# Heads of 8 in an attention kernel: single steps against woven rounds of two, with the PSUM banks shared out anew

## The reference, cut to what matters

```
q, k, v = x @ Wq, ctx @ Wk, ctx @ Wv        # 16 heads of width 8
p       = softmax(q @ k.T * 8 ** -0.5)      # 256 queries x 1601 keys
out     = concat_heads(p @ v) @ Wo + x
```

## Time and profile before

| | |
|---|---|
| time, median of 3 runs | 7700.89 us (7677.93 to 7725.98) |
| the profiled execution | 7682.88 us, its span 7681.1 us |
| heads-of-8 stages, first exp to last, `a0` | 1478 us |
| the same, `a1` and `a3` | 1185 and 1183 us |
| busy over the span: TensorE, VectorE, ScalarE, POOL | 90%, 77%, 65%, 30% |
| largest group: exp, L691, 5248 instructions | 2820.6 us busy |

### The profile page before, as it was taken

One profiled execution on the slowest core, in us unless ns is written; L12 is line 12 of the kernel. 1 busy time (PEld: TensorE's weight loads), 2 busy tenths in 40 slices (PEclk: granted clock), 3 DMA queues, 4 the chain that ended last, 5 costly groups with the idle time before them and its releaser, 6 DMA issues. The chain is left out here.

```text
span 7681.1 us, 186319 instructions
## 1 busy us (share of the span) xinstructions
PE 6915.8 (90%) x73814; PEld 3126.6 (41%) x73814; DVE 5883.2 (77%) x12879; ACT 4973.1 (65%) x9846; POOL 2317.5 (30%) x2368
## 2 busy tenths in 40 slices
PE   7999999978999998888769999999997799999979
PEld 3333333343333333344434444444444433333335
DVE  6888888846899997687657777777774488989955
ACT  5877878734888886455336666666654168888842
POOL 2222222111221211154435555555554112112100
PEclk9999999987999999898879999999999589999989
DMA  4444434103434341100110000000001144343400
GB/s 110 95 88 88 91 88 91 43 27 76 100 73 103 88 86 44 28 18 15 37 27 10 6 10 9 7 10 9 5 5 49 29 101 98 75 103 85 86 26 12
DMA packets 318293, 412.96 MB, mean 54 GB/s; under 512 B 56437, under 2 KB 237957, under 8 KB 317432
## 3 DMA queue, kind: packets, MB, share of 16 engines
q1 hardware_dynamic: 308818, 395.82, 22.4%
q10 hardware_dynamic: 8614, 5.21, 0.2%
HBM read 225.41 MB, written 174.66 MB: 52 GB/s over the span
## 5 line engine op out<-in xcount | busy, mean ns | idle before, releaser
L691 ACT ACTIVATE a_probs<-scores_ps 128x512 f32<-128x512 f32 (+2 forms) x5248 | 2820.6, 591 | 364.0 <-PE scores_ps L611 271.2
L750 DVE TENSOR_REDUCE a_unit_max<-bank 128x1 f32<-128x512 f32 x3072 | 2003.6, 683 | 193.1 <-PE bank L598 158.3
L628 PE MATMUL bank<-a_probs,a_v_sb 128*9 128x256 f32 (+1 forms) x20992 | 1626.6, 382 | 29.2 <-ACT a_out_sb L698 20.1
L1302 ACT ACTIVATE cross_probs<-scores_ps 128x512 f32<-128x512 f32 (+1 forms) x1792 | 868.6, 571 | 592.0 <-PE scores_ps L1197 592.0
L611 PE MATMUL scores_ps<-a_stack 49*128 49x256 bf16 (+1 forms) x10496 | 1140.7, 276 | 57.1 <-ACT a_probs L691 54.6
L1384 DVE TENSOR_REDUCE cross_unit_max<-bank 128x1 f32<-128x512 f32 x1536 | 979.2, 685 | 253.3 <-PE bank L1183 250.1
L750 DVE TENSOR_REDUCE a_unit_max<-scores_ps 128x1 f32<-128x512 f32 x1536 | 1049.7, 683 | 145.2 <-PE scores_ps L598 128.5
L598 PE MATMUL bank<-a_stack 48*128 48x512 bf16 (+2 forms) x3413 | 1046.6, 375 | 6.4 <-DMA a_stack<-a_stack_dram 1.3
L1468 POOL TENSOR_TENSOR cross_added<-cross_probs 128x1024 f32<-128x1024 f32 x384 | 905.5, 2358 | 327.9 <-PE bank L1230 240.0
L611 PEld LDWEIGHTS scores_ps<-a_stack 49*128 49x128 bf16 (+1 forms) x10496 | 375.3, 96 | 995.7 <-ACT a_probs L691 832.2
L515 POOL CAST a_parts<-a_qk 128x512 bf16<-128x512 f32 (+3 forms) x225 | 117.7, 523 | 1903.8 <-ACT a_qk L710 1813.3
(11 more groups left out here) (420 smaller groups left out, 10025.3 us busy)
## 6 DMA issues: line engine op xcount, KB each, us to landing
a_stack_dram<-a_parts SPq DMA_DIRECT2D x288, 400.2 KB, 4.2
a_stack<-a_stack_dram SPq DMA_DIRECT2D x256, 348.2 KB, 7.9
a_stack<-a_stack_dram SPq DMA_DIRECT2D x128, 444.2 KB, 10.0
a_ctxT<-in_ctxT SPq DMA_DIRECT2D x48, 400.2 KB, 4.8
a_stack_dram<-a_parts SPq DMA_DIRECT2D x288, 64.0 KB, 2.3
a_stack_dram<-a_parts SPq DMA_DIRECT2D x96, 128.0 KB, 2.2
f_x<-x_after_dram SPq DMA_DIRECT2D x32, 256.0 KB, 3.7
x_after_dram<-a_res SPq DMA_DIRECT2D x48, 128.0 KB, 4.5
```

The source lines that it names most:

```text
L628: ins = pe.matmul(out_bank[32 * h:32 * h + V8, q0:TOK], v[0:n, e.t, 4 * e.g + h, :], A.probs[0:n, held, o + q0:o + TOK], start=(e.t == 0), ...
L691: act.activation(by_pair(A.probs[0:n, b, a * 512:(a + 1) * 512])[:, :, q0:TOK], by_pair(score_bank[(2 * e.i + a) % 3][0:n, :])[:, :, q0:TO ...
L750: ins = dve.tensor_reduce(unit_max[:, e.g % 2, qt, 2 * a + j, c:c + 1], bank[:, 0:e.s.chunks[c][1]], AX.X, ALU.max)
L1302: act.activation(probs[0:n, b, h, 0:m, :].rearrange("p m q -> p (m q)"), score_bank[h][0:n, 0:m * TOK], ACT.Exp, scale=scale).then_inc(S[" ...
```

## The change

`segment8` is replaced by `plan8`, which lays the events of all batches on one line of steps and then goes through it in rounds of two steps:

- **Rounds.** A round has the scores of both steps, then the pv of the two steps before them, then at most one side job. pv comes thus in sets of two back to back (three at the end of quads 0 and 2, one in the round after).
- **Weaving.** Scores are issued by row half. Between the two score matmuls of one half stands the matmul of one unit on the other half (`beside`). The units of a pair change places (`k ^ 1`) for that.
- **Banks.** Four score banks in turn; a half's scores wait for the exp four before. The remaining three banks beside `out_bank` (`turn_bank`) serve units and side jobs in one rotation, in the order of issue: each waits until whatever stood three before it in the list was taken out.
- **Side jobs** take an even slot each (`free`). `first` jobs (`k_cross`, `v_cross`) stand after the scores and before the pv, and are taken out in the same round. `last` jobs (all others) stand after the pv, and are taken out in the next round, after its first exp (`late`).
- **Lead.** Units run 12 steps ahead (`SPACE8`), not 4; the projections for the next batch begin 10 steps earlier (`AHEAD8`) than the batch before. `negmax` has two buffers.

```diff
+    def first(n, kind, b, **k):
+        n = free(n)
+        e = put(n, "first", kind, b, **k)
+        evac(n, "first", e)
+        return n
+
+    def last(n, kind, b, **k):
+        n = free(n)
+        e = put(n, "last", kind, b, **k)
+        evac(n + 2, "late", e)
+        return n
...
+    for n0 in range(-end - 24, max(n for n, _ in at) + 2, 2):
+        core = 0 <= n0 < total
+        for half in range(2):
+            n = n0 + half
+            units = units_at.get(n, [])
+            for a in range(2):
+                mine = units[a * len(units) // 2:(a + 1) * len(units) // 2]
+                if core:
+                    s, g, t = steps[n % end]
+                    plan += [Ev("scores", s=s, g=g, t=t, i=n, part=a), Ev("exp", s=s, g=g, t=t, i=n, part=a)]
+                    plan[-2].batch = plan[-1].batch = n // end
+                    plan[-2].beside = None
+                    if mine and mine[0].s.row_tile(mine[0].k) != a:
+                        plan[-2].beside = mine[0]
+                        mine[0].woven = True
+                plan += mine
+                if half == 0 and a == 0:
+                    plan += at.get((n0, "late"), [])
+            if half == 1:
+                plan += at.get((n0, "first"), [])
+        if 0 <= n0 <= total:
+            upto = n0 + int(n0 < total and steps[n0 % end][2] == steps[n0 % end][0].T - 1)
+            for i in range(gone, upto):
+                s, g, t = steps[i % end]
+                plan.append(Ev("pv", s=s, g=g, t=t, i=i))
+                plan[-1].batch = i // end
+            gone = max(gone, upto)
+        plan += at.get((n0, "rest"), []) + at.get((n0, "last"), [])
...
+    held = [None, None, None]
+    for k, e in enumerate(order):
+        e.bank, e.bank_units, e.bank_jobs = k % 3, 0, 0
+        if held[e.bank]:
+            e.bank_units = held[e.bank].u + 1 if held[e.bank].kind == "unit" else 0
+            e.bank_jobs = held[e.bank].n + 1 if held[e.bank].kind != "unit" else 0
+        held[e.bank] = e
...
-        score_bank = [G.S4[:, 0, 0, :], G.S4[:, 0, 1, :], G.S4[:, 1, 0, :]]
-        max_bank = [G.S4[:, 1, 1, :], G.bank[2][:, :], G.bank[3][:, :]]
+        score_bank = [G.S4[:, 0, 0, :], G.S4[:, 0, 1, :], G.S4[:, 1, 0, :], G.S4[:, 1, 1, :]]
+        turn_bank = [G.bank[1][:, :], G.bank[2][:, :], G.bank[3][:, :]]
...
+                    if 2 * e.i + a >= 4:
+                        pe.wait_ge(S["probs"], 2 * e.i + a - 3)
...
                     for j in range(2):
-                        for a in range(2):
-                            ins = pe.matmul(score_bank[(2 * e.i + a) % 3][0:n, j * TOK + q0:(j + 1) * TOK],
-                                            stack[p][rows(a, 49), 2 * e.g + j, k0:k0 + n],
-                                            stack[p][rows(a, 49), 2 * e.g + j, c0 + q0:c0 + TOK], start=True, stop=True)
-                            if j == 1:
-                                ins.then_inc(S[f"scores{a}"], 1)
+                        ins = pe.matmul(score_bank[(2 * e.i + a) % 4][0:n, j * TOK + q0:(j + 1) * TOK],
+                                        stack[b][rows(a, 49), 2 * e.g + j, k0:k0 + n],
+                                        stack[b][rows(a, 49), 2 * e.g + j, c0 + q0:c0 + TOK], start=True, stop=True)
+                        if j == 0 and e.beside:
+                            unit(e.beside)
+                    ins.then_inc(S[f"scores{a}"], 1)
```

More of the change, by code:

```diff
@@ L39 @@
 V8 = 9
-LAG8 = 3
 def key_tiles(nk):
@@ L231, in segment8 @@
     end = len(steps)
+    total = BATCH * end
     at, units_at = {}, {}
[L234 to L258, removed]
@@ new lines, in free @@
+    def free(n):
+        n += n % 2
+        while n in taken:
+            n += 2
+        taken.add(n)
+        return n
[8 more added lines that the diff above has]
+        evac(n + 2, "late", e)
+        return n
+    for b in range(BATCH):
+        base = b * end
+        windows = [(cross, g, base + cross.T * (g - 1) - SPACE8, base + cross.T * g - SPACE8) for g in range(QUADS)]
+        windows[0] = (cross, 0, base - SPACE8 - cross.T, base - SPACE8)
+        at_own = base + cross.T * (QUADS - 1) - SPACE8
+        for s in own:
+            for g in range(QUADS):
+                windows.append((s, g, at_own, at_own + s.T))
+                at_own += s.T
+        for s, g, start, stop in windows:
+            n_units = cross.UNITS if s is cross else s.NU
+            for k in range(n_units):
+                e = Ev("unit", s=s, g=g, k=k ^ 1, r=int(k == n_units - 1))
+                e.batch = b
+                units_at.setdefault(start + k * (stop - start) // n_units, []).append(e)
+            n = last(stop, "turn", b, s=s, g=g)
+            put(n + 2, "late", "row", b, s=s, g=g)
@@ L270, in segment8 @@
+    for b in range(BATCH):
+        base = b * end
+        before = base - end
+        ahead = before - AHEAD8
+        put(ahead - 14, "rest", "ln_stats", b)
+        put(ahead - 14, "rest", "ln_rstd", b)
+        put(ahead - 12, "rest", "ln_apply", b)
+        last(ahead - 10, "x_turned", b)
+        n = ahead - 2
+        for c in range(len(cross.chunks)):
+            n = first(n + 2, "k_cross", b, c=c)
+            put(n, "rest", "split", b, j=c)
+        n = last(n + 2, "q", b)
         if own:
-            put(8, "k_own")
@@ L278, in segment8 @@
+        n = before + 8
         for j in range((cross.T + 3) // 4):
-            put(12 + 2 * j, "v_cross", j=j)
-        if own:
-            put(20, "v_own")
-    for quad in range(QUADS * len(sources)):
-        done = sum(s.T for s in sources for g in range(QUADS) if sources.index(s) * QUADS + g <= quad)
-        n = done + LAG8 + 2
-        late = n >= end
-        if with_tail if late else with_core:
-            put(TAIL_OF8[False]["quad_out"] if late and not own else n - late * end, "quad_out", quad=quad, nxt=late)
@@ L303, in segment8 @@
-    for e in plan:
-        e.cur = cur
-        e.batch = cur - 1 if e.kind in ("pv", "quad_out") and e.nxt else cur + 1 if e.nxt else cur
+            n = first(n + 2, "v_cross", b, j=j)
+        done = base
+        n = base
+        for quad in range(QUADS * len(sources)):
+            done += sources[quad // QUADS].T
+            n = last(max(n + 2, done + 2 - done % 2), "quad_out", b, quad=quad)
+        put(base + 20, "rest", "x_res", b)
+        n = last(n + 4, "heads_turned", b)
+        last(n + 2, "proj", b)
```

237 lines of the change are left out of this document (126 added, 111 removed).

## The result

| | before | after |
|---|---|---|
| time, median of 4 runs each, on one chip | 7707.98 us (7677.93 to 7725.98) | 8529.08 us (8522.82 to 8615.08) |
| ratio after / before, 95% interval | | 1.108 [1.101, 1.116] |
| the profiled execution | 7682.88 us, span 7681.1 | 8615.08 us, span 8613.3 |
| first exp of `a0` after | 74.2 us | 94.0 us |
| `a0`, first exp to last | 1478 us | 1926 us |

The changed kernel is 821 us slower by the medians, where I had forecast 710 on 7700.

What follows compares the result with a forecast made beforehand. Before, plain steps go at VectorE's 1.20 us; after, a three-bank loop bounds rounds at 2.50. +410 (`a1`, `a3`), +285 (`a0`) and +24 (starts) make +719 on 7681, 8400; with the runs' median 8410 us, 8 in 10 within 7880 to 8600.

Steps and rivals of the forecast that it cites:

- The loop of the three banks: Every round: fourth unit waits for the first's bank until 1.15 us, 1.35 follow; at least 2.50 against 2.40 for two steps.
- VectorE paces and the saved drains count: Rival for all three stages: fourth unit follows the first by under some 1.05 us, time about 7410; chance 0.06.
- Side jobs in `a1`: Per batch of `a1`: `last` jobs' own time 4.2 us, their bank waits 7.2, `first` jobs' waits 9.5.
- The sum for a batch: `a1` and `a3`: bank rounds 65.0 us plus side jobs and VectorE's rest give 86.9 us a batch, +12.8.
- the layer norm: VectorE's two 0.81 us instructions and the statistics, inside the loop, less 0.4 idle: +1.9 us a batch.
- the ends of quads: Rounds shortened by tail units: -0.5 us a batch; the wait at a quad's end goes away, inside 2.50.
- The clock: Rival: clock falls too, a round some 1.3 us longer in a quarter of `a0`'s 480 rounds, +156, 8570 us; chance 0.06.
- `a0`: +285 forecast: Stage `a0`: 110.2 us a batch, +17.8, 16 times, +285 us in all.
- The meeting of five turns with the DMAs of `stack`: In `a0`: `stack` DMAs costed at nothing; if their lead's cover goes, some us a batch, kept for the range.
- Starts of stages: At each stage's start 16 more units precede the first exp, less its end's gain: some +8 us, three times, +24.

Runs made afterwards that it cites:

- e_evacfirst: Changed kernel with a last job's evacuation moved ahead of the next round's first exp and first unit maximum: 8100 us, ratio 1.053 to the kernel before.
- e_pvstep: Changed kernel with one set of pv behind each step's scores, not two at the round's end: 8099 us, ratio 1.053 to the kernel before.
- e_four_evac: Changed kernel with three score banks, four banks in the shared rotation, and evacuation ahead of the first exp: 8070 us, ratio 1.049 to the kernel before.
- e_filler: Changed kernel with four extra copies of score matmuls a round, ahead of the second step's scores: 8520 us, ratio 1.109 to the kernel before.
- e_apart: Changed kernel with three score banks, three for units alone and one for side jobs alone: 8107 us, ratio 1.057 to the kernel before.

## Why the prediction was right, and where it was off

**The loop of the three banks: right.** Forecast 2.50 us for a plain round, the fourth unit at 1.15 and 1.35 behind it; measured 2.47, the fourth unit at 1.17 and 1.30. `e_evacfirst` leaves this loop standing, with four score banks, and its rounds without a job still take 2.48; `e_pvstep` opens it with the same banks, and they take 2.20 where no job of the round before holds them up; `e_four_evac` takes it away and finds the next one. "VectorE paces and the saved drains count" asked for a fourth unit under 1.05 us, and of the 71 plain rounds in `a1` none has one.

**Side jobs in `a1`: most are right within 0.1 us.** In one batch of `a1` (2401 to 2487 us): a `turn` alone 2.79, forecast 2.77; `quad_out` after a `turn` 3.32, forecast 2.50 + 0.52 + 0.33 = 3.35; full `first` jobs 3.83 to 3.90 where no `last` job stands before them, forecast 3.89. VectorE is busy 67.6 of 86.0 us, 79%, as written ("under 80%").

**The sum for a batch: 2.3 us too high.** 86.9 forecast, 84.6 at full clock. The term that failed is the layer norm, 1.9 us from two instructions of 0.81 in the loop. VectorE's own lines in `a1`, before and after, with the least, median and longest in ns:

```profile
L147 DVE TENSOR_SCALAR a_xn<-a_x,a_ln_mv,a_ln_rs x30: 337/808/1116, 1847.2 to 2892.9; 128x128 f32<-128x128 f32 x30
```

```profile
L146 DVE TENSOR_SCALAR a_xn<-a_x,a_ln_mv,a_ln_rs x28: 335/340/344, 2368.8 to 3511.1; 128x128 f32<-128x128 f32 x28
```

In the kernel before, POOL was at its splits of `a_qk` beside each of the 30, in the changed kernel POOL did nothing beside any of the 28; the new order has parted them. The rounds with the layer norm (3.44 and 2.97) are within 0.05 of my prices without it. The other part is the ends of quads: the four rounds with tail units and the two `turn` rounds with one set of pv take together 1.0 us less than my prices, where the term for them was 0.5. For 32 batches the 2.3 us are 74 us too many.

**The clock: given 0.06, and it came, beside the loop, not in its place.** The mis-sized step is this one. In the changed kernel's `a1` one batch without a drop and one with:

```profile
3204.20:3288.80 84.60, 70.67 (x818) 29.99 (x814) 67.12 (x126) 62.27 (x123) 14.47 (x23) 1.00 0.35 79
2755.90:2846.60 90.70, 77.48 (x819) 32.17 (x814) 67.25 (x126) 62.25 (x123) 14.00 (x21) 0.91 0.33 73
```

The clock of 0.91 is 17.1 us at the lower level, and the batch is 6.1 us longer: 0.36 us lost for each us at 1.2 GHz (before, two kinds of batch in `a0`, 91.5 and 97.8 us, give 0.37). The three stages have 847 us more at the lower level than before, so at that price some 300 us. In `a1` and `a3` the price is borne out: 0.32 to 0.47 over their batches with such time, and `e_filler`'s numbers there come near it. In `a0` it may be too high, since `e_filler` gained 51 us for 307 us there, 0.17 for each with the cost of its copies inside. I had treated the clock as an alternative to the sum, and weighed it by one row of before. But the sum itself said that TensorE would stand idle for a fifth of each round (1.98 of 2.50 us), so the two belonged together.

The Trainium skill, "TensorE: Matmul & The Clock Gate", section Terms, prices throttled time at its length times 1 - K/N, which is half. Here it was 0.36. That part of the time is waiting, which takes as long at either level, would explain it; no run shows this apart.

**`a0`: +285 forecast, +448 measured.** 618 of its 1926 us are at the lower clock, 542 more than before, which at 0.17 to 0.36 is 92 to 195 us. The meeting of five turns with the DMAs of `stack` is 66 to 81 us between profiles, part of it again through the clock (157 us less of it). Both are in the 163 us missing; their shares are not settled, because no run changes the one without the other.

**Starts of stages: +8 forecast.** The first exp of `a0` came 20 us later, that of `a1` 15. I had counted 16 units more ahead of it and let the stage's end give part of it back; in the profile the distance from `a0`'s last exp to `a1`'s first grew instead (284 to 300 us).

**Taken together** the errors partly cancel: batches 74 us too high, stage starts some 20 to 30 too low, clock and `a0`'s DMAs at nothing, where what is left of the 821 us, 821 - 719 + 74 - 25 = 151, is theirs. The forecast of 8410 lies 119 under the measured 8529: 102 of these are the growth (821 against 719), 7 the median of before, which a fourth run raised from 7701 to 7708, and 10 were lost in rounding, since 7701 and 719 are 8420. That it came so near is in part luck. The direction and its cause, a loop of banks that no engine's busy time shows, were shown by `e_apart`, `e_evacfirst` and `e_pvstep`, each of which takes away one wait and gets 420 to 430 us. Together the last two, with one score bank given to the rotation, get 718. How much of each is the clock's share stays open.

## What to carry to other kernels

Before issues are gathered into longer rounds, count the banks of each kind that one round fills: if it fills more than there are, the round is at least matmul to reader (0.41), reader (0.68), semaphore (0.05), plus all that stands behind the waiting issue. What opened that loop here was other work of the same engine in the gap, as pv after each step; a bank taken from the other kind only moved the loop there. A shared rotation makes every user wait for the slowest one's evacuation, so take that out ahead of long instructions of the same engine. An idle share that a sum predicts for TensorE should also be priced at the lower clock, on top of the sum.

## What the runs showed of the hardware that was not expected

- VectorE's `tensor_scalar` of 128 x 128 in f32 took 0.34 us with POOL idle, 28 times of 28 in the changed kernel's `a1`, and 0.81 us in the median beside POOL's casts and subtractions, 30 times in the `a1` of before (29 of them 0.75 or longer).
- A microsecond at half the granted clock cost 0.36 us here (17.1 us low, batch 84.6 to 90.7), and matmuls that only fill waits halved the time at the low clock (961 to 463 us) with no measurable gain in the program's time (ratio 1.109 against 1.108).
- A DMA issue of 0.52 us on ScalarE's queue straight after an activation kept its next activation back by 0.59 to 0.60 us. Issued after four exps of the round, it delayed none: it went out at 2437.35 beside exps that were queued ahead of it and started at their usual 0.58 us apiece (2436.55, and two later 2437.71), and was over at 2437.87, while the next exp waited for its scores until 2439.11. Behind it no exp was ready, so this does not show what it would do to one.
- Bringing the matmuls of scores and of a unit together on the two row halves gained 0.01 us a step in the changed kernel (85.2 against 84.6 us a batch). Where TensorE sets the pace, a woven step takes 1.09 us and one of before 1.14; no run has this kernel unwoven, so the 0.05 is not shown to be the weaving's.
